# Last normalising sweep of a GNN and mixture-of-experts kernel: weights handed over in turned layout, deeper buffers, rows normalised by ACT

## What is computed

```python
x = x + gnn(_layernorm(x), W0..b2, src, dst)          # three attention layers
# ffn on xf = _layernorm(x):
router_logits = jnp.einsum('th,eh->te', xf, Wr)        # Wr (8, 768)
topk_vals, topk_idx = jax.lax.top_k(router_logits, 2)
routing_weights = jax.nn.softmax(topk_vals, axis=-1)
h = gelu(jnp.einsum('th,efh->etf', xf, Wi) + bi)       # Wi (8, 192, 768)
expert_out = jnp.einsum('etf,ehf->eth', h, Wo) + bo    # Wo (8, 768, 192)
x = x + sum over the two experts of routing_weight * expert_out
```

## Time and profile before

| | us |
|---|---|
| median of three runs | 3523.0 |
| the profiled execution | 3531.71 |
| its span (first to last instruction in the profile) | 3530.1 |

### The profile page before, as it was taken

The page is one execution under the profiler, slowest core; times in us unless marked ns, Lnnn a source line. Parts: engine busy times, 40 slices in busy tenths (PEclk is TensorE's granted clock), DMA queues, the critical chain, the costliest instruction groups (busy, mean ns, idle before and its releaser), DMA issues.

```text
span 3530.1 us, 59081 instructions
## 1 busy us (share of the span) xinstructions
PE 2860.2 (81%) x14522; PEld 1988.6 (56%) x14526; DVE 2172.1 (62%) x4157; ACT 1258.5 (36%) x2606; POOL 1484.8 (42%) x1494
## 2 busy tenths in 40 slices
PE   0796999998979798999887978889889444499994
PEld 0684555555568555555556855555555344477663
DVE  8646888888877588888886745455555444412111
ACT  0222555555544355555554422222323111011110
POOL 1003666666600366666650036666665000024331
PEclk9997999999989899999998989999999555579997
DMA  3234899999834588988883458888987565136666
GB/s 109 97 114 151 295 295 296 293 296 298 264 130 161 193 294 294 297 291 298 294 259 130 160 190 287 287 299 292 295 291 257 208 225 191 47 76 126 122 120 167
DMA packets 214505, 775.59 MB, mean 220 GB/s; under 512 B 33734, under 2 KB 73071, under 8 KB 214222
## 3 DMA queue, kind: packets, MB, share of 16 engines
q0 software_dynamic: 121520, 585.03, 52.3%
q1 hardware_dynamic: 75166, 136.38, 12.8%
q10 hardware_dynamic: 17744, 53.26, 3.9%
HBM read 673.45 MB, written 111.48 MB: 222 GB/s over the span
## 4 chain that ended last, share of the span: by engine, by line
PE 31%; DVE 25%; issue 20%; DMA 12%; ACT 4%; another core or an unknown queue 4%; POOL 1%; ACTq 1%; DVEq 1%; SPq 1%; POOLq 0%
PE PS L864 19%; DMA x_kept<-arena,target_of 6%; DVE arena L1245 5%; PE PS L794 4%; DMA arena<-table 3%; DVE parts L1262 2%; PE PS L796 2%; DMA arena<-table,src_k 2%; PE PS L839 1%; DVE arena L1133 1%; DVE arena L1148 1%; DVE arena L1149 1%; DVE W L1245 1%; PE PS L782 1%
## 5 line engine op out<-in xcount | busy, mean ns | idle before, releaser
L533 POOL DMA_INDIRECT arena<-table,src_k x945 | 964.5, 1021 | 511.9 <-PE PS L864 237.5
L864 PE MATMUL PS<-arena,S 128*128 128x384 f32 (+1 forms) x1848 | 697.4, 508 | 52.7 <-issue 33.2
L1245 DVE TENSOR_TENSOR arena<-arena,PS 128x768 f32<-128x768 f32 x630 | 585.9, 946 | 0.9 <-issue 0.9
L864 PEld LDWEIGHTS PS<-arena,S 128*128 128x128 f32 x1848 | 337.7, 192 | 261.3 <-issue 114.9
L533 POOL DMA_INDIRECT W<-table,src_k x315 | 312.8, 993 | 165.9 <-PE PS L864 76.1
L794 PE MATMUL PS<-W_split,S 128*128 128x512 f32 x900 | 357.5, 415 | 30.2 <-DVE xT_rest L1172 29.4
L864 PE MATMUL PS<-parts,S 128*128 128x384 f32 (+2 forms) x1344 | 338.2, 373 | 52.1 <-issue 45.6
L864 PE MATMUL PS<-arena,S_weighted 128*128 128x384 f32 (+1 forms) x840 | 317.9, 513 | 47.6 <-issue 34.1
L839 PEld LDWEIGHTS PS<-erp,ST_b 128*128 128x128 bf16 x3780 | 195.5, 97 | 254.3 <-issue 186.3
L499 POOL DMA_DIRECT2D table<-arena x75 | 40.9, 545 | 663.2 <-ACT arena L595 651.5
L683 ACT ACTIVATE apart<-iota_row,dst_k 128x128 f32<-128x128 f32 x840 | 265.1, 389 | 88.9 <-issue 57.1
(11 more groups left out here) (248 smaller groups left out, 4714.8 us busy)
## 6 DMA issues: line engine op xcount, KB each, us to landing
local_b<-local SPq DMA_DIRECT2D x252, 160.0 KB
mixed<-sums ACTq DMA_DIRECT2D x75, 384.0 KB
arena<-mixed SPq DMA_DIRECT2D x75, 384.0 KB, 3.7
arena<-table SPq DMA_DIRECT2D x75, 384.0 KB, 5.1
table<-arena POOLq DMA_DIRECT2D x50, 390.0 KB, 3.6
arena<-in_x SPq DMA_DIRECT2D x48, 384.0 KB, 4.1
arena<-table,src_k POOLq DMA_INDIRECT x945
table<-arena POOLq DMA_DIRECT2D x25, 384.5 KB, 4.8
```

The costliest lines, as they stand in the source:

```text
L533: nc.gpsimd.indirect_dma_start(edge_row(l, k % U)[:, 0:D + HEADS[l]], None, table[l][:, :], bass.IndirectOffsetOnAxis(src_k[:, k:k + 1].bi ...
L864: o = nc.tensor.matmul(flat[:, bass.ds(odd * 1024 + 512 * c, n)], onehot, row[:, c * HALF:c * HALF + n], start=False, stop=True, skip_grou ...
L1245: nc.vector.tensor_tensor(z, z, a, ALU.mult).then_inc(s_msg, 1)
```

## The change

1. The host hands over Wr, Wi and Wo already laid out for the matmuls. Wr goes straight to `WrT` at the start; Wi to `WiT` by one DMA of 4.7 MB, issued on SP between layer 2's node sweep and its `local_b` loads; Wo to `WoT` by one DMA of 4.7 MB, issued on SP behind the last sweep's loads. `raw_weights`, `pieces`, `load_weights`, `copy_weights`, `turn_weights` and the turning of Wr are gone. `WiT` moves to the end of `W`, over layers 1 and 2, since layer 0's part holds gathered rows until the edge sweep ends.
2. The last sweep is written out block by block, without a hardware loop, with its own buffers in `arena`: 4 for `mixed` (which also holds the sum), 3 for `table`, 3 for x, 3 for the normalised rows, 2 for the turned rows; PSUM has two pairs of banks for turned rows. Its first loads wait for the edge sweep's last matmul, and those of `mixed` only for the store of their block.
3. The rows are normalised by ACT (`Identity` with scale 1/sd and bias -mean/sd); DVE computes the bias (one 128x1 instruction more) and does not run the 128x768 `tensor_scalar`. DVE does the previous block's `bound` between its additions.

```diff
+            for b in range(NB):                                   # SP
+                rows = LAST if b == NB - 1 else P
+                if b >= LN_ADD:
+                    sp.wait_ge(s_summed, b - LN_ADD + 1)
+                arrived = s_ln_in[b % LN_IN]
+                sp.dma_start(ln_table(b), table[2][b * P:(b + 1) * P, 0:D]).then_inc(arrived, 16)
+                sp.dma_start(ln_x(b)[0:rows], x[b * P:b * P + rows, :]).then_inc(arrived, 16)
+                sp.wait_ge(s_sums_st, 16 * (NB * 2 + b + 2))
+                if b >= LN_IN:
+                    sp.wait_ge(*ln_stored(s_kept_x2, b - LN_IN, LN_IN))
+                    sp.wait_ge(s_turnable, b - LN_IN + 1)
+                sp.dma_start(ln_sum(b), mixed[2][b * P:(b + 1) * P, :]).then_inc(arrived, 16)
+            sp.dma_start(WoT[0:FH, :, :, :, :], ffn["Wo"]).then_inc(s_cload, 16)
-            sweep_nodes(sp, [(load(3), 0), (load_weights, 0)])
...
+            def normalise(b):                                      # ACT
+                act.wait_ge(s_bound, b + 1)
+                if b >= LN_OUT:
+                    act.wait_ge(*ln_stored(s_kept, b - LN_OUT, LN_OUT))
+                    act.wait_ge(s_xTp, NB * 3 + b - LN_OUT + 1)
+                nc.scalar.activation(ln_out(b), ln_sum(b), ACT.Identity, scale=stats[:, b % 2, 15:16],
+                                     bias=stats[:, b % 2, 14:15]).then_inc(s_turnable, 1)
...
+            for b in range(NB + 1):
+                if b:
+                    normalise(b - 1)
+                if b < NB:
+                    keep_x2(b)
+                    deviation(b)
+                if b:
+                    turned_rows(b - 1)
...
+            for b in range(NB + 1):                                # PE
+                if b < NB:
+                    turn(b)
+                if b:
+                    logits(b - 1)
-            sweep_nodes(pe, [(turn, 1), (logits, 0), (turn_weights, 0)])
-            pe.wait_ge(s_wcp, PIECES)
...
+            pe.wait_ge(s_cload, 16 * 4)                            # ahead of the experts
...
+            def summed(b):                                         # DVE
+                u = ln_sum(b)
+                dve.wait_ge(s_ln_in[b % LN_IN], 16 * 3 * (b // LN_IN + 1))
+                link(nc.vector.scalar_tensor_tensor(out=u, in0=u, scalar=den_flat(2)[:, b:b + 1], in1=ln_table(b),
+                                                    op0=ALU.mult, op1=ALU.add))
+                link(nc.vector.tensor_tensor(u, u, bias[:, :], ALU.add))
+                if b:
+                    bound(b - 1)
+                nc.vector.tensor_tensor(u, u, ln_x(b), ALU.add).then_inc(s_summed, 1)
+                dve.wait_ge(s_summed, b + 1)
+                if b >= 2:
+                    dve.wait_ge(s_turnable, b - 1)
+                st = stats[:, b % 2, :]
+                nc.vector.bn_stats(st[:, 0:6], u[:, 0:HALF])
+                link(nc.vector.bn_stats(st[:, 6:12], u[:, HALF:D]))
+                nc.vector.bn_aggr(st[:, 12:14], st[:, 0:12]).then_inc(s_stat, 1)
```

More of the change, by code:

```diff
@@ L301, in rows_f, with ln_buf, ln_sum, ln_table @@
             return arena[:, 4 * 2 * P:8 * 2 * P]
[L303 to L314, removed]
+        def ln_buf(k):
+            return arena[:, k * D:(k + 1) * D]
+        def ln_sum(b):
+            return ln_buf(b % LN_IN)
+        def ln_table(b):
+            return ln_buf(LN_IN + b % LN_ADD)
+        def ln_x(b):
+            return ln_buf(LN_IN + LN_ADD + b % LN_ADD)
+        def ln_out(b):
+            return ln_buf(LN_IN + 2 * LN_ADD + b % LN_OUT)
+        def ln_xT(b):
+            return ln_buf(LN_IN + 2 * LN_ADD + LN_OUT + b % 2)
+        def ln_stored(sems, b, count):
+            return sems[b % count], 16 * (b // count + 1)
         def f32(t):
@@ L424, in _ @@
                     sp.dma_start(bias[:, :], gnn[3 * 0 + l - 1]["b"].partition_broadcast(P)).then_inc(s_bias, 16)
[L425 to L434, removed]
+                sweep_nodes(sp, [(load(l), 0)])
@@ new lines, in _ @@
+                if l == 2:
+                    sp.wait_ge(s_W_rest, 3 * KC)
+                    sp.dma_start(WiT, ffn["Wi"]).then_inc(s_cload, 16)
+                sp.wait_ge(s_local, 16 * 4)
+                for g in range(NG):
+                    used = NG * l + max(0, g - NBUF + 1)
+                    if used:
+                        sp.wait_ge(s_ST, used)
+                    sp.dma_start(local_b[:, g % NBUF, :], local[g * G:(g + 1) * G, :].rearrange("g e -> (g e)").partition_broadcast(P)
+                                 ).then_inc(s_lb[g % NBUF], 16)
@@ L437, in _ @@
+            sp.dma_start(bi_row, ffn["bi"].rearrange("e f -> (e f)").rearrange("(o n) -> o n", o=1)).then_inc(s_cload, 16)
             sp.dma_start(WoT[FH:FH + 1, :, :, 1, :],
                          ffn["bo"].rearrange("(o e) (c d) -> o e c d", o=1, c=2)).then_inc(s_cload, 16)
[L439 to L451, removed]
@@ L889, in _, with turn @@
                 edge_sweep(l)
[L892 to L899, removed]
+            def turn(b):
+                pe.wait_ge(s_turnable, b + 1)
+                if b >= 2:
+                    pe.wait_ge(s_xT, NB * 3 + b - 1)
+                for k in range(KC):
+                    o = nc.tensor.transpose(flat_banks(2 * (b % 2))[:, k * P:(k + 1) * P], ln_out(b)[:, k * P:(k + 1) * P],
+                                            ident[:, :])
+                o.then_inc(s_xTp, 1)
@@ L1338, in _ @@
+                nc.vector.bn_aggr(st[:, 12:14], st[:, 0:12]).then_inc(s_stat, 1)
+            dve.wait_ge(s_den, NB * 3)
             denominators(2)
-            sweep_nodes(dve, [(begin, 2)], dc, 2 * 6)
+            for b in range(NB):
+                summed(b)
+            bound(NB - 1)
             lg, pairs, t, best = routing("lg"), routing("pairs"), routing("t"), routing("best")
```

140 lines of the change are left out of this document (63 added, 77 removed).

## The result

| | before | after |
|---|---|---|
| median, us | 3523.08 (3518.81 to 3529.8, 4 runs) | 3379.12 (3375.28 to 3384.05, 4 runs) |
| ratio | | 0.959, 95% interval 0.9571 to 0.961 |
| profiled execution, us | 3531.71 | 3379.89 |
| from ACT's last `den` copy to the first routing instruction | 292.4 us | 147.1 us |

A forecast was written before the change was run, and what follows sets the result against it. It took the DMA engines to become the last sweep's bound at 340 GB/s: 2748.3 + 24 x 5.8 + 14 = 2901.5 instead of 3034.9, 133.4 us less, giving 3389.6 us; range 3364 to 3422.

The forecast's parts named there:

- What bounds the kernel: Last sweep: bound by waiting, 11.2 us a block, in a circle of `table` loads, weight loads and PE's turnings.
- Deep enough rings: Last sweep's new buffers: rings take 3.4 to 3.6 us a block, at most 6.1 with doubled landing times, so don't bind.
- DMA engines as the bound: Last sweep after the change: 1.966 MB a block at 340 GB/s, 5.8 us, above DVE's 4.95; chance 0.52.
- DVE's block: DVE's instructions for one block of the last sweep: 4.95 us together, with normalising's 0.68 us gone.
- The tail and the last block: End of the last sweep: last block priced like the others, 5.8 us; then a tail of 14 us; Wo's load costs nothing.
- Handover: Into the last sweep: first node load near 2742.4, DVE starting 5.9 us later at 2748.3 instead of 2753.88.
- ACT's normalising: Last sweep: one more 128x768 instruction a block on ACT, about 0.79 us; ACT's 2.2 us stays under DVE's, costing nothing.
- DVE is the bound: Rival for the last sweep: transfers keep near 404 GB/s, a block costs DVE's 4.95 us, kernel 3369 us; chance 0.18.
- Slow mix: Rival for the last sweep: sustained reads and writes at 284 GB/s, 6.92 us a block, kernel 3416 us; chance 0.21.
- no depth: Rival: SP's in-order queue leaves one block ahead in the last sweep, 10.9 us a block, kernel 3512 us; chance 0.04.
- slow loads: Rival: whole-matrix Wi and Wo loads delay layer 2's edge sweep and the experts; at 150 us landing, 3549 us; chance 0.02.
- One by one: Rival: a last-sweep block's five transfers each pay 2.8 us landing in turn, 14 us a block, kernel 3586 us; chance 0.01.

The follow-up runs named there:

- e1: Kernel before with only the weights changed: host layouts, Wi and Wo as one DMA each, no pieces or turning; ratio 1.0009 to the kernel before.
- e11: Changed kernel with the store of x2 put back late, behind ACT's square root and copy of turned rows; ratio 0.9623 to the kernel before.
- e2: Changed kernel with all the last sweep's buffers two deep instead of 4, 3, 3; ratio 0.973 to the kernel before.
- e8: Changed kernel with the addition of the last layer's bias left out; ratio 0.958 to the kernel before.
- e3: Changed kernel with Wo's load waiting until all 25 blocks are normalised; ratio 0.9541 to the kernel before.
- e4: Changed kernel with the last block's 53-row load of x split into 48 and 5 rows; ratio 0.9559 to the kernel before.
- e6: Changed kernel with both Wo's load after the last normalising and the 53-row load split; 3362.7 us, ratio 0.9549 to the kernel before.
- e7: Changed kernel with DVE normalising the rows again instead of ACT; 3382.22 us, ratio 0.9595 to the kernel before.

## Why the prediction was right, point by point

- **What bounds the kernel: half right.** I named one ring, over SP, PE's turnings and the loads. It was there, and the change removes it, but e1 shows that its removal alone gives nothing: a second ring, over DVE, ACT's late store of x2 and its landing, had nearly the same length, 10.5 us. The step that failed is the reading of the earlier trace rows as *the* circle. The forecast held because the change removes the second ring too, and that is luck, since I had not seen it: `keep_x2` stands first in ACT's turn, a part of the diff to which I gave no price, and four buffers cover even a late one (e11).
- **Deep enough rings: right.** I had 3.4 to 3.6 us a block, 6.1 at most with doubled landing times. The landing of the store of x2 more than doubled (median 7.1 us for 2.8), that of the loads hardly changed (7.0 to 8.2 for 7.4), and the rings still did not bind. My ring left out that a load of `mixed` also waits for ACT's normalising of block b - 4; at four deep this costs nothing, at two it is the ring that binds (e2, 7.45 us).
- **DMA engines as the bound: right, the rate mis-sized.** 340 GB/s was the term; it is 413 to 415 for 80 us and more [windows of after and of e8], so 4.73 us a block in place of 5.8. My row of 340 GB/s began with the DMA engines empty; its last 6 us are at 262 to 408. Over 23 blocks this is 24.7 us too much in the forecast.
- **DVE's block: 4.95 forecast, 4.44 measured.** From start to start the new 128x1 instruction takes 0.08 us, not 0.18, the last addition 0.99, not 1.11, the moments 1.05, not 1.17, and the next block starts 0.13 us behind the start of the last instruction, not 0.25. With this number right the bound would have been the same.
- **The tail and the last block: missed.** I took the last block for one like the others, though the wait of 19.4 us stood at it in the earlier trace rows. It cost 15.1 us in place of 5.8, and the tail 17.0 in place of 14. Two causes share this: the load of 53 rows on one engine (6.5 us of DVE's wait are left in e3), and Wo's load, which I costed at nothing and which slows the last transfers (e3 and e4); with both gone the last block takes 4.4 us and the tail 13.7 (e6). Wo's load had 111 us of cover for itself; what it did to its neighbours I did not ask.
- **Handover: right.** From the `den` copy to DVE's first sum 6.3 us, forecast 5.8.
- **Sum.** 24.7 us too long in the pitch, 9.3 + 3.0 + 0.5 too short elsewhere: 11.9 us net, in which the errors of both signs partly cancel. By the stretch from `den` to the routing I forecast 159.0 us, and it is 147.1.
- **ACT's normalising: right** that it costs nothing on ACT (1.03 us, not 0.79) and that DVE's saving matters little; e7 puts it at 3 to 6 us.
- **The rivals.** "DVE is the bound" came as near in time (3369) as the forecast did, 10 us, by the wrong engine: e8 and e7 show that DVE is 0.3 us a block from it. "Slow mix" is refuted by 413 GB/s of reads and writes together, "no depth" by the pitch, "slow loads" by the layer 2 edge sweep and the experts, which start no later than before. "One by one" is refuted by the same 413 GB/s, reached with transfers of 384 KB; 1 MiB in a DMA, which the prediction quotes from the Trainium skill, was not needed for it.

## What to carry to other kernels

When a wait is removed and nothing is gained, look at the small wait beside it: two rings of the same length share one stretch of time, and the profile books most of it to the one that comes last (111.9 us here, against 17.6). In a pipeline of loads and stores, issue the store as soon as its data is there, ahead of the waits for the next block, and ask of each buffer who reads it last, since the next load waits for that reader too (in e2 it was the normalising, not the store). A ragged last tile wants its own look: a DMA of 53 rows ran on one engine of sixteen, and a load that nothing waits for soon can still hold up the last stores beside it, so it should start behind them.

## What the runs showed that I had not expected

- The two whole-matrix loads run at different rates. Wi, 128 partitions with 36,864 bytes each, moves at 400 GB/s over 12 us, stores beside it included, and at 453 in this row of the changed kernel, whose share of 1.10 says that the view overstates it:

```profile
2046.00:2054.00 8.00, 7.91 (x48) 6.77 (x48) 6.15 (x9) 3.30 (x4) 0.54 (x1) 1.00 1.10 453
```

  Wo, 96 partitions with 49,152 bytes each, moves at 235 in e3, with the DMA engines as busy and almost nothing beside it:

```profile
2612.00:2630.00 18.00, 4.70 (x19) 4.07 (x18) 12.44 (x49) 0.45 (x2) 0.00 (x0) 0.50 1.00 235
```

  Whether the 96 partitions or the longer runs make this was not tried.
- The page "DMA: Bandwidth & Descriptors" of the Trainium skill (section Specifications) gives one core about 358 GB/s of device memory, half of what two cores share; the sweep holds 413 for 85 us with this core alone at work, so the trace disagrees with that figure as a limit here.
- Chips differ by 8% with this kernel, and not in the last sweep: the changed sweep's pitch, 4.73 us, and its rate, 413 GB/s, are the same in e3 on the chip of 3258.6 us as in the first profile. The difference shows in the gathers of the edge sweeps, 332 GB/s in e1's profile against 284 in the earlier trace rows:

```profile
2000.00:2470.00 470.00, 448.07 (x2459) 285.87 (x2458) 281.73 (x924) 158.96 (x349) 352.91 (x346) 1.00 0.94 332
```
